# A macaron layer on one core: the down product in two steps, four hid buffers, one exps buffer, and shifted due times

## What is computed

```python
def expert_step(acc, w):                       # 8 experts, HIDDEN 128, FFN 512
    wg, wu, wd = w
    h = jax.nn.silu(x @ wg) * (x @ wu)
    return (acc + h @ wd, None)
...
scores = einsum('bhqd,bhkd->bhqk', q, k)       # 16 heads of 8, rotary q and k
scores = scores + einsum('bhqd,qkd->bhqk', q, rel)   # rel = rel_emb[clipped distance, +-32]
attn = softmax(where(causal, scores, -1e18))
ctx = einsum('bhqk,bhkd->bhqd', attn, v) + einsum('bhqk,qkd->bhqd', attn, rel)
...
x = x + 0.5 * ffn(layernorm(x))
x = x + attention(layernorm(x))
x = x + 0.5 * ffn(layernorm(x))
```

## Time and profile before

| | |
|---|---|
| median of 3 runs | 1497.45 us (1497.14 to 1497.76) |
| the profiled execution | 1493.65 us |
| its span, first to last instruction | 1491.8 us |
| TensorE, union of its matmuls | 1409.3 us, 94% |
| VectorE busy | 1306.3 us, 88% |
| ScalarE busy | 1120.3 us, 75% |
| GpSimd busy | 1087.5 us, 73% |

### The profile page before, as it was taken

How to read it: one execution, slowest core, us unless ns; L and a number is a source line. 1 busy time by engine, 2 the same in 40 slices (tenths; PEclk the granted TensorE clock), 3 DMA queues, 4 the chain that set the end, 5 groups by cost and what they waited for, 6 DMA issues and landing times.

```text
span 1491.8 us, 28938 instructions
## 1 busy us (share of the span) xinstructions
PE 1409.3 (94%) x8632; PEld 1074.1 (72%) x8632; DVE 1306.3 (88%) x2541; ACT 1120.3 (75%) x2642; POOL 1087.5 (73%) x956
## 2 busy tenths in 40 slices
PE   8999899999999999899999999999999899999898
PEld 6777677777776777577767767767776677777686
DVE  5888899999999899898999988999999799989665
ACT  6657778878787787788778777777878578877555
POOL 7867687787677777777768777787777677667555
PEclk9999999999999999999999999999999899999999
DMA  6305999999999999999999999999999999997300
GB/s 201 114 29 141 182 208 170 189 200 176 191 177 177 179 176 190 184 175 167 185 186 186 193 167 175 163 222 173 172 184 155 186 174 181 173 172 136 56 1 8
DMA packets 716380, 241.42 MB, mean 162 GB/s; under 512 B 650304, under 2 KB 679744, under 8 KB 716224
## 3 DMA queue, kind: packets, MB, share of 16 engines
q1 hardware_dynamic: 556224, 172.45, 68.0%
q10 hardware_dynamic: 160000, 67.13, 21.8%
HBM read 77.34 MB, written 69.86 MB: 99 GB/s over the span
## 4 chain that ended last, share of the span: by engine, by line
PE 41%; DVE 22%; ACT 11%; issue 9%; DMA 6%; POOL 5%; SPq 4%; ACTq 2%; POOLq 0%; DVEq 0%
PE work L677 8%; PE work L678 7%; PE work L679 7%; DVE hid L1026 4%; DVE hid L1032 4%; DVE negmax L1128 4%; DVE work L1123 4%; PE acc L755 4%; PE acc L758 4%; PE acc L756 3%; DMA probs_t<-probs 3%; SPq L655 3%; POOL hid_lo L1178 3%; PE work L806 2%; ACT work L926 2%
## 5 line engine op out<-in xcount | busy, mean ns | idle before, releaser
L1178 POOL TENSOR_TENSOR hid_lo<-hid,hid_hi 128x512 fp32r<-128x512 f32 x512 | 662.8, 1300 | 265.6 <-ACT hid_hi L881 262.3
L1026 DVE SCALAR_TENSOR_TENSOR hid<-hid,work 128x512 f32<-128x512 f32 x512 | 346.8, 681 | 86.0 <-ACT hid L876 84.7
L881 ACT ACTIVATE hid_hi<-hid 128x512 fp32r<-128x512 f32 x512 | 324.9, 637 | 119.0 <-DVE hid L1032 62.0
L876 ACT ACTIVATE hid<-work 128x512 f32<-128x512 f32 x512 | 305.5, 603 | 118.3 <-PE work L679 71.3
L1032 DVE TENSOR_TENSOR hid<-hid,work 128x512 f32<-128x512 f32 x512 | 348.0, 681 | 7.1 <-PE work L679 1.9
L677 PE MATMUL work<-xt,wg 128*128 128x512 f32 x512 | 215.3, 421 | 16.2 <-DVE hid L1026 7.5
L1193 POOL TENSOR_TENSOR probs<-exps,probs 128x512 f16<-128x512 f32 (+1 forms) x160 | 171.1, 1069 | 73.0 <-ACT probs L938 72.8
L677 PE MATMUL work<-xt,wu 128*128 128x512 f32 x512 | 211.8, 414 | 13.0 <-DVE hid L1032 7.5
L1128 DVE TENSOR_REDUCE negmax<-work 128x1 f32<-128x384 f32 (+3 forms) x352 | 220.8, 636 | 1.0
L1123 DVE TENSOR_TENSOR work<-work,rel_win 128x160 f32<-128x160 f32 (+2 forms) x352 | 190.6, 552 | 25.4 <-PE work L806 24.2
L755 PE MATMUL acc<-hid_hi,wd 128*128 128x512 f32 x512 | 211.1, 412 | 0.4 <-ACT hid_hi L881 0.3
(11 more groups left out here) (97 smaller groups left out, 2191.4 us busy)
## 6 DMA issues: line engine op xcount, KB each, us to landing
rel_win<-rel_window_scratch ACTq DMA_DIRECT2D x128, 320.0 KB, 4.7
prob_window_scratch<-probs SPq DMA_DIRECT2D x384, 80.0 KB, 3.6
q_scratch<-rope SPq DMA_DIRECT2D x16, 512.0 KB, 4.1
qq<-q_scratch ACTq DMA_DIRECT2D x32, 256.0 KB
rel_window_scratch<-g_s SPq DMA_DIRECT2D x32, 256.0 KB, 3.3
k_scratch<-rope SPq DMA_DIRECT2D x16, 512.0 KB, 4.8
kk<-k_scratch ACTq DMA_DIRECT2D x32, 256.0 KB
prob_window_scratch<-probs SPq DMA_DIRECT2D x32, 256.0 KB, 3.5
```

Source lines behind the costliest of these rows:

```text
L876: act.activation(hid[:, arg % HB, :], work[bank_of["gate", arg]][:, :], ACT.Tanh, scale=0.5).then_inc(s_tanh, 1)
L881: act.mul(hid_hi[:, arg % 2, :], hid[:, arg % HB, :], 1.0).then_inc(s_hhi, 1)
L1026: dve.scalar_tensor_tensor(out=hid[:, arg % HB, :], in0=hid[:, arg % HB, :], scalar=1.0, in1=work[bank_of["gate", arg]][:, :], op0=ALU.add ...
L1178: pool.tensor_tensor(hid_lo[:, arg % 2, :], hid[:, arg % HB, :], hid_hi[:, arg % 2, :].bitcast(F32), ALU.subtract).then_inc(s_hlo, 1)
```

## The change

- `down` keeps the two matmuls on `hid_hi`. The third, on `hid_lo`, becomes a step of its own, `down_lo`, which may stand anywhere later in TensorE's list. Each has its semaphore (`s_down`, `s_dlo`). `hi` of chunk n now waits for `down` of n - 2 and for `lo` of n - 2; `lo` of chunk n waits for `down_lo` of n - 2; the copy of `acc` waits for the last `down_lo`.
- `HB` goes from 3 to 4: `tanh` of chunk n waits for `lo` of n - 4. `EB` goes from 2 to 1: `exp` of a lent task waits for `p_lent` of the lent task before it.
- `near` runs over the same elements in another order: heads innermost, columns outside, where it was columns innermost.
- A table `LATER` is added to the due times by the name of the step, 42 names from -5.8 to +5.0.

```diff
-    HB = 3
+    HB = 4
...
-    EB = 2
+    EB = 1
...
+    LATER = {"acc": -0.9, "band_turn": -3.1, "band_values": -2.8, "down_lo": 5.0, "gated": 0.1, "ln_hi": 0.3,
...
-        steps[name, arg] = (engine, takes, LANDS[engine] if lands is None else lands, time,
+        steps[name, arg] = (engine, takes, LANDS[engine] if lands is None else lands, time + LATER.get(name, 0.0),
...
-        step("ACT", act_wide(L), at + 3, "hi", n, ("product", n), ("down", back(n, 2)))
-        step("POOL", 1.25, at + 3.7, "lo", n, ("hi", n))
-        step("PE", 0.695, at + 5, "down", n, ("lo", n), split[2], ("acc", p - 1 if k == 0 and p else None))
+        step("ACT", act_wide(L), at + 3, "hi", n, ("product", n), ("down", back(n, 2)),
+             ("lo", back(n, 2)))
+        step("POOL", 1.25, at + 3.7, "lo", n, ("hi", n), ("down_lo", back(n, 2)))
+        step("PE", 0.463, at + 4, "down", n, ("hi", n), split[2], ("acc", p - 1 if k == 0 and p else None))
+        step("PE", 0.232, at + 5, "down_lo", n, ("down", n), ("lo", n))
...
-                    pe.matmul(acc[:, :], wd[:, LO, e, cols], hid_hi[:, arg % 2, :], start=False, stop=False)
+                    pe.matmul(acc[:, :], wd[:, LO, e, cols], hid_hi[:, arg % 2, :], start=False,
+                              stop=False).then_inc(s_down, 1)
+                if name == "down_lo":
                     pe.wait_ge(s_hlo, arg + 1)
                     pe.matmul(acc[:, :], wd[:, HI, e, cols], hid_lo[:, arg % 2, :], start=False,
-                              stop=(k == CH - 1)).then_inc(s_down, 1)
+                              stop=(k == CH - 1)).then_inc(s_dlo, 1)
...
                     wait(act, s_down, arg - 1)
+                    wait(act, s_hlo, arg - 1)
...
-                    act.wait_ge(s_down, CH * (arg + 1))
+                    act.wait_ge(s_dlo, CH * (arg + 1))
...
-                    near = heads[:, :, i * P - R + lo:keys]
+                    near = heads[:, :, i * P - R + lo:keys].rearrange("p a c -> p c a")
...
-                    dve.tensor_tensor(near, near, rel_win[:, quad % WB, lo:W, places[0]:places[-1] + 1].rearrange(
-                        "p c a -> p a c"), ALU.add).then_inc(s_near, 1)
+                    dve.tensor_tensor(near, near, rel_win[:, quad % WB, lo:W, places[0]:places[-1] + 1],
+                                      ALU.add).then_inc(s_near, 1)
...
                     pool.wait_ge(s_hhi, arg + 1)
+                    wait(pool, s_dlo, arg - 1)
```

More of the change, by code:

```diff
@@ L90, in macaron_kernel @@
     LANDS = {"PE": 0.35, "ACT": 0.35, "DVE": 0.35, "POOL": 0.35, "SP": 2.6}
+    LATER = {"acc": -0.9, "band_turn": -3.1, "band_values": -2.8, "down_lo": 5.0, "gated": 0.1, "ln_hi": 0.3,
+             "ln_lo": 2.7, "ln_rstd": -0.9, "ln_scaled": 3.3, "ln_stats": -0.3, "ln_turned": -0.2, "lo": 0.8,
+             "load_band": -0.9, "load_k": 1.5, "load_window": 0.8, "near": 2.9, "outproj": 0.1, "p_hi": -3.1,
+             "p_lent": -1.0, "p_lo": 1.5, "p_turn": -0.2, "product": 0.5, "project": -4.4, "q_pad": 1.3, "qk_hi":
+             -5.8, "qk_store": 0.9, "qrel": -3.9, "qrel_store": 0.3, "recip": 1.4, "recip_copy": 0.9,
+             "recip_turned": 0.7, "recip_wide": 2.8, "scale": -1.0, "scores": -2.3, "split_lo": -2.5,
+             "store_band": -5.8, "sum": -1.3, "sum_turned": 1.3, "tanh": -3.1, "up": 1.4, "v_split": 1.7,
+             "values": -3.0}
     def step(engine, takes, time, name, arg, *after, lands=None):
@@ L177, in macaron_kernel @@
         end = PART * (p + 1) + 4.6
-        step("ACT", act_wide(L), end - 9, "acc", p, ("down", CH * (p + 1) - 1))
+        step("ACT", act_wide(L), end - 9, "acc", p, ("down_lo", CH * (p + 1) - 1))
         step("PE", 0.44, end - 9, "sum_turned", p, ("acc", p))
@@ L310, in macaron_kernel @@
         _, takes, lands, *_ = steps[key]
-        if name in ("gate", "up", "down", "project") and (start > clock["PE"] or after_short):
+        if name in ("gate", "up", "down", "down_lo", "project") and (start > clock["PE"] or after_short):
             takes += 0.1
@@ L443, in macaron_kernel @@
         s_hlo = sem("hid_lo_ready")
-        s_down = sem("down_done")
+        s_down = sem("down_of_hi_done")
+        s_dlo = sem("down_of_lo_done")
         s_acc = sem("acc_copied")
@@ L725, in _ @@
             for name, arg in order:
-                if name in ("gate", "up", "down"):
+                if name in ("gate", "up", "down", "down_lo"):
                     p, k = arg // CH, arg % CH
```

## The result

The changed kernel takes 1445.74 us (median of four runs, 1443.11 to 1446.95) against 1497.3 us before on the same chip: a ratio of 0.9654 with a 95% interval of 0.9637 to 0.9670, so 51.6 us less. I had forecast 1467.5 us, 30 us less, with a range from 1446.0. The profiled execution took 1443.11 us, its span is 1441.3 us.

The account below looks back on a forecast made before the run. No engine was taken as full: VectorE (91.3% busy) and TensorE, near nine tenths, hold each other up. Near -14, down and buffers -20, extra step +3, one exps +1, due times 0: 1497.45 - 30 = 1467.5 us, range 1446 to 1503.

Parts of the forecast that it names:

- Near, the size on VectorE: VectorE's near with heads innermost: contiguous or paired reads of rel_win save 12.9 + 16.1 = 29 us of VectorE's time.
- the three shapes: VectorE's near by task size: (1085 - 440) / (512 - 160) = 1.83 ns an element before the change.
- Near, the share that reaches the end: Of the 29 us saved on VectorE in near, half reaches the end: 14 us less.
- the chain's share: near's line has some 60 us of its 191.2 us busy on the chain, share 0.31, giving 9 us.
- Down in two steps and the buffers: Feed-forward: fewer waits of ScalarE and TensorE's weight loads, 20 us less; with added costs of 3 and 1 us.
- One step more, one exps buffer: TensorE's down_lo begins its own group, +3 us; exp of a lent task waits for the previous p_lent, +1 us.
- Due times at 0: The planner's shifted due times move everything a little: taken as 0, bounds 10 us less to 20 us more.
- Rival 1: TensorE's down, nine matmuls nearer to up, waits for hi: 1508 us; slower had 0.14, mostly by this.
- a sign of being wrong: A new wait of TensorE's down matmul for hid_hi, of tens of us.
- Rival 2: near gains nothing because of PSUM stride and waits turn into others: 1492 us; little change, 1486 to 1500, had 0.16.
- Rival 3: VectorE is the bound outright, so 29 and 40 us count in full: 1432 us; faster than 1446 had 0.08.

Follow-up runs that it names:

- stand-in: Each DMA transpose of probabilities and bands replaced by two plain DMAs of half the bytes, turning left out; kernel before 1471.2 us, changed kernel 1427.2 us.
- plain_near_structure: plain_after3 without the table of due-time shifts, so the new near walk, down in two steps and new buffer numbers; 1487.1 us.
- fixed lists: plain_after3 with every engine's list kept: three hid buffers at run time, 1445.7 us; or hi waiting for down_lo of n - 2, 1459.6 us.
- plain_before3: The kernel before the change, with each DMA transpose replaced by two plain DMAs of half the bytes; 1471.2 us.
- plain_after3: The changed kernel, with each DMA transpose replaced by two plain DMAs of half the bytes; 1427.2 us.

## Why the prediction was right and wrong

**Near, the size on VectorE: right.** I had 29 us from the slope of the three shapes; the rows after say 28.9, and 0.69 and 0.49 us where I wrote 0.69 and 0.48. The walk over PSUM with a stride, which no row showed, costs nothing here that can be seen: 691 ns for 512 elements against 681 for the contiguous `product`. The rule of the Trainium skill's "SBUF — State Buffer", Specifications, agrees: pairs and fours within 16 bytes run at full rate and single elements, 438 ns for 160 as before, don't. The rule of the Trainium skill's "PSUM — Partial Sum Buffer", Specifications, is about matmuls and doesn't carry over to VectorE in these rows.

**Near, the share that reaches the end: right in size.** 12 us alone in the stand-in, 14 forecast. With both other parts in it is 4 (open). 12 us lie between the 9 by the chain's share and the 14 that I took, and the noise doesn't tell them apart, so the half was a guess that came out. That VectorE is the fullest engine can't be the whole reason: in the changed kernel it is fuller (93.0%), and `near` is worth no more.

**Down in two steps and the buffers: the number right, on a condition that I didn't see.** -20 + 3 + 1 = -16 was forecast, -16.7 is measured on top of `near` and the due times. But alone it is +23. ScalarE's waits went as I said (80.8 to 21.3 us), and TensorE's for the banks went further (66.4 to 22.7; I had let 22.6 go and 43.7 went), but part of that is the table's doing, which takes 22 us of them by itself. And waits that go are no gain by themselves: in plain_near_structure ScalarE's are gone too, and the time is 28 us longer. At fixed lists the two waits cost 18.5 and 32.4 us, each more than the 16 for all. So -16 agreeing with -16.7 is in part luck.

**One step more, one exps buffer: not seen.** The first matmul of `down` went from 412 to 420 ns and that on `hid_lo` from 397 to 405 ns, 8 ns x 512 = 4 us each. The first matmuls of `gate` and `up` became shorter by more, 421 to 405 and 414 to 403 ns, so no net cost is seen, and no run has this term by itself. Of `exp` no wait for GpSimd's `probs` is listed after.

**Due times at 0, bounds -10 to +20 us: this step failed.** "They move everything a little and have no price in the rows. ... I take 0." They bring 15 to 16 us on the old structure, outside the bound of 10, and 60 on the new one. Of the 21.6 us by which the forecast of 30 fell short, these 15 us are the main part; 7.6 us more are what the stand-in does not show (below). Two errors are in it. First, I priced the structure as if its lists were the old ones with one step moved; but the planner makes all lists anew, and the diff's structure without the table was one of the plans that could come out, 28 us worse than none of it. A price of 0 for another order of the same structure has no ground when the structure's own price assumes a good order. Second, the bound: of the 44 us of bank waits that I left over I let 10 us count at the most. On the old structure the table took 22 us of such waits away (67.6 to 45.5), and 16 us came out at the end.

**Rival 1, TensorE waits for `hi`: the wait is there, its price was wrong.** 26.8 us of the weight loads and 8.6 us of the matmul in the changed kernel are 35.4 us, or 0.07 us a chunk. I had said that at 0.06 us the gain is gone, and had named such a wait as a sign of being wrong; the gain is larger than forecast all the same, so these waits don't count in full. Nor are they what the structure alone loses by: its weight loads wait 23.1 us for `hi`. Where the wait on `down_lo` is put back they are 62.2 us and the time is 32.4 us longer, but there `hi` is late for another reason than the rival's. **Rival 2** (`near` gains nothing because of PSUM) fell with the rows of `near`. **Rival 3** (1432 us, VectorE the bound outright) was nearer to the time than the forecast (14 us off, not 22), but not for its reason: `near` was worth 12 or less, not 29.

**From the stand-in to the kernel** 7.6 us are left over (51.6 against 44). In the trace of before TensorE stands 16.9 us for turned probabilities; after, the row has 2.7 us:

```profile
  issue: 42.3, 110
  DMA probs_t<-probs: 2.7, 4
```

In the stand-in the same row has 2.2 us in plain_before3 and 0.6 in plain_after3. So the kernel itself lost 14.2 us of this wait by the change and the stand-in 1.6, which fits 7.6 us; but no run held it apart, so it is argued and not shown.

## What to carry to other kernels

When a change goes through a planner, price the plan, not the step: the same edit cost 23 us with one set of priorities and brought 17 with another, and even a shuffled table beat the untouched one. So test a structural edit with a handful of different orders before judging it, compare when the same chunk ends in both, which here put 20 of 28 us into one stretch, and test each of its waits at fixed lists, where both cost about half of the waiting time that came with them, though they sit on an engine that is not the bound. For a tensor_tensor on VectorE with one operand in SBUF, put the dimension that is contiguous in SBUF innermost and let PSUM have the stride; that is measured here for fp32 with strides of 128 and 256 elements.

## What the runs showed of the hardware that I had not expected

- VectorE read and wrote PSUM with an innermost stride of 128 fp32 elements in 691 ns for 512 and of 256 in 492 ns for 320, which is 1.04 ns an element, as for contiguous ones; an innermost stride of four elements in SBUF had cost 1085 and 732 ns.
- Two plain DMAs in place of one DMA transpose of the same bytes, on the same queue, made the kernel before 27 us faster (1497.9 to 1471.2; 19 to 38 us by the interval). The issuing queue gains nothing: a transpose takes 1.24 us of it, and a plain half 0.62 (medians). The median time to landing is 4.4 us for the transpose and 3.3 us for the pair's 128 KB halves, and TensorE's wait for them fell from 16.9 to 2.2 us:

```profile
probs_t<-probs SPq DMA_DIRECT2D x448, 128.0 KB, 3.3
...
probs_t<-probs SPq DMA_DIRECT2D x256, 96.0 KB, 3.0
```

- From a stall of TensorE of 2.4 us on (672.1 to 674.5 us in plain_near_structure) its granted clock was 0.50 for some 22 us, in which it stood three times more, for 8.6 us in all. A chain of such stalls is paid in waiting and in clock.
